# Two changes of order in a loop over routed experts: unit numbers kept in registers, activations cast ahead of rows

## The chip, the cores and the metric

One core of one Trainium2 chip. The metric is the device time of one launch in microseconds (us); smaller is better.

## What is computed

Two layers, each an attention-like block and a feed-forward block with residuals, over `x` of 8 x 256 x 512. The change touches only the last block, a mixture of 32 experts with four picked per token (T = 2048 tokens, H = 512, I = 256), all in 32-bit:

```python
scores = softmax(x @ gate_w.T); topk_w, topk_ids = top_k(scores, 4)   # weights normalized
buf[e, pos] = x[tok]                    # each expert's tokens, up to a capacity
gu = einsum('ech,ehf->ecf', buf, w13);  g, u = split(gu, 2)
act = silu(g) * u
eo = einsum('eci,eih->ech', act, w2)
routed = zeros.at[tok].add(eo[...] * topk_w)
shared = silu(x @ shared_gate_w) * (x @ shared_up_w) @ shared_down_w
out = residual + routed + shared
```

## The kernel before

Everything ahead of the expert loop (both attentions, the first feed-forward block, routing, the shared expert) is as it was and ends near 695 us. Then comes the loop, with a queue of its own written out by hand for each engine; the engines keep step by semaphores alone.

The routed rows are cut into units of 128 rows of one expert; a table in SBUF holds for each unit its expert (in a code that is divided by `STRIDE`) and the column of the row weights. A round handles two units, `s` = 0 and 1, called the first and the second row here. There are 40 rounds; two rounds (`q` = 0 and 1) make one turn of the loop, so rounds are called even and odd. The number of turns is read at run time.

Each 32-bit operand is split into a high part (a cast) and a low part (what the cast lost, `lo_part`, line 1778), and a product is the sum of three: high x high, low x high, high x low.

In round `i`, TensorE does in this order:

- `turn_act(i,0)` (tile `x_ab`, line 2605): transposes the first unit's activation (2 matmuls)
- `turn` of both rows of round `i+1` (tile `x_xb`, line 2587): 8 transposes of the gathered rows
- `down(i,0)` (tile `x_o`, lines 2616, 2617, 2622), with `turn_act(i,1)` between its first products and the others, then `down(i,1)`: 12 matmuls
- `up(i+1,0)` and `up(i+1,1)` (tile `x_h`, lines 2597 to 2599): 12 matmuls each

`up` waits at its head for the low part of the turned row, `down` for the high part of the turned activation, `turn_act` for the activation itself. Which expert's weights a pass uses is in a register of TensorE's queue: `experts_of` loads two unit codes from SBUF (`code_of`, line 1785). A load on a queue is an instruction of that queue; the engine's work is issued by the same queue, ahead of the engine and in order.

ScalarE, per round (`round_of`, line 2731): two silus (line 2712), then `turned_act`, the cast of a turned activation (line 2717), and `turned`, for a turned row: `weigh`, which loads a column number into a register (line 2500) and copies the row's weight (line 2700), and then the row's cast (line 2707). Before the change these stand as activation 0, row 0, activation 1, row 1. At the end both outputs of `down` are copied out of PSUM (line 2747).

VectorE, per round (`round_of`, line 2821): `gated`, silu times up times the row's weight, for each unit (line 2805); the low parts of activation and row, in ScalarE's order; and the split of a new expert's weights where a unit opens one: the first half at the end of a round (`first_half`, lines 2776 and 1778), the second half in the next round between its two `gated` (`second_half`, lines 2782 and 1778). So the second activation of a round stands behind that split.

POOL gathers the rows two rounds ahead (line 1794) and adds the results to memory (line 2521). SP loads the experts' weights two experts ahead (lines 1790 and 1799).

Of the kernel before, what the change touches and what calls it, by code (L numbers as in the profile page):

```python
# [49 lines left out]
NE, TOPK, FI = 32, 4, 256  # L50
# [1675 lines left out]
def experts(nc, st, sem, sbuf, psum, scratch_dram, y_d, a, x, ident, powers, lns, count_row, tail, rows, out):  # L1726
# [50 lines left out]
    def lo_part(dst, src, hi):  # L1777
        return nc.vector.tensor_tensor(dst, src, hi.bitcast(F32), ALU.subtract)  # L1778

    def last_of(eng):  # L1780
        return eng.value_load(last_round[0:1, 0:1], min_val=1, max_val=(T * TOPK // P + NE) // 4 - 1)

    def code_of(eng, j):

        return eng.value_load(unit_tile[0:1, ds(j, 1)], min_val=0, max_val=NE * STRIDE - 1)
# [16 lines left out]
    with ExitStack() as sr:  # L1802
        xl, r, nw, rr, norm = rows.xl, rows.r, rows.nw, rows.rr, rows.norm
# [46 lines left out]
        first = sbuf(sr, "rt_first", [P, 1])  # L1850
# [606 lines left out]
    with ExitStack() as se:  # L2457
# [40 lines left out]
        def column_of(eng, j):  # L2498

            return eng.value_load(unit_col[0:1, ds(j, 1)], min_val=0, max_val=NE)  # L2500
# [81 lines left out]
        def _(pe):  # L2582
            def turn(n, q, s):

                pe.wait_ge(got[q][s], 16 * n + 16)
                for k in range(KD):
                    last = nc.tensor.transpose(xbank[s][:, k * P:(k + 1) * P], xg[q][s][:, k * P:(k + 1) * P], ident[:])  # L2587
                last.then_inc(xt_ps, 1)

            def up(i, s, e):  # L2590

                at = ds(e % SPLIT, 1)
                hi, lo = xt[s]
                pe.wait_ge(w13_lo, e + 1)
                pe.wait_ge(xt_lo, 2 * i + s + 1)
                for k in range(KD):
                    nc.tensor.matmul(hbank[s], hi[:, k, :], w13p[0][:, at, k, :], start=k == 0, stop=False)  # L2597
                    nc.tensor.matmul(hbank[s], hi[:, k, :], w13p[1][:, at, k, :], start=False, stop=False)  # L2598
                    last = nc.tensor.matmul(hbank[s], lo[:, k, :], w13p[0][:, at, k, :], start=False, stop=k == KD - 1)  # L2599
                last.then_inc(h_ps, 1)  # L2600

            def turn_act(i, s):
                pe.wait_ge(x_av_ready, OPEN + 2 * i + s + 1)
                for f in range(KI):
                    last = nc.tensor.transpose(abank[s][:, f * P:(f + 1) * P], av[s][:, f * P:(f + 1) * P], ident[:])  # L2605
                last.then_inc(at_ps, 1)
# [20 lines left out]
            def experts_of(i):  # L2627
                return [code_of(pe, 2 * i + s) // STRIDE for s in range(2)]

            def rest(n, q, e, following=None):  # L2630

                i = 2 * n + q
                turn_act(i, 0)
                if following:
                    turn(n + q, 1 - q, 0)
                    turn(n + q, 1 - q, 1)
                down(i, 0, e[0], between=lambda: turn_act(i, 1))
                down(i, 1, e[1])
                if following:
                    for s in range(2):  # L2640
                        up(i + 1, s, following[s])

            n, first = pe_opens
            for s in range(2):
                up(0, s, first[s])
            with pe.Fori(0, n) as i:
                for q in range(2):
                    rest(i, q, experts_of(2 * i + q), experts_of(2 * i + q + 1))
            rest(n, 0, experts_of(2 * n), experts_of(2 * n + 1))
            rest(n, 1, experts_of(2 * n + 1))  # L2650

            def tile_of(t):
                return banks[t // 2 % 4][:, t % 2]
# [43 lines left out]
        @block.scalar  # L2697
        def _(act):
            def weigh(i, q, s):
                nc.scalar.copy(rw[:, s:s + 1], xg[q][s][:, ds(D + column_of(act, 2 * i + s), 1)]).then_inc(rw_ready, 1)  # L2700

            def turned(i, q, s):
                j = 2 * i + s
                act.wait_ge(xt_ps, OPEN + j + 1)
                act.wait_ge(x_av_ready, OPEN + j - 1)
                weigh(i, q, s)
                nc.scalar.copy(xt[s][0][:], xbank[s].rearrange("p (k n) -> p k n", n=P)).then_inc(xt_hi, 1)  # L2707

            def silu(i, s):
                act.wait_ge(h_ps, 2 * i + s + 1)  # L2710
                act.wait_ge(x_av_ready, OPEN + 2 * i + s - 1)
                nc.scalar.activation(gs[s], hbank[s][:, 0:FI], ACT.Silu).then_inc(gs_ready, 1)  # L2712

            def turned_act(i, s):
                act.wait_ge(at_ps, OPEN + 2 * i + s + 1)
                act.wait_ge(eo_ps, OPEN + 2 * i + s - 1)
                nc.scalar.copy(avt[s][0][:], abank[s].rearrange("p (f n) -> p f n", n=P)).then_inc(at_hi, 1)

            def weights_2(e):
                act.wait_ge(x_w_ready, e + 1)  # L2720
                nc.scalar.copy(w2p[0][:, e], w2[:, e]).then_inc(w2_hi, 1)  # L2721

            act.sem_inc(eo_sb, OPEN)
            weights_2(0)
            act.wait_ge(xt_ps, OPEN + 2)
            nc.scalar.copy(xt[1][0][:], xbank[1].rearrange("p (k n) -> p k n", n=P)).then_inc(xt_hi, 1)
            for s in range(2):
                weigh(0, 0, s)
            weights_2(1)

            def round_of(i, q, more=True, before=None):
                silu(i, 0)
                silu(i, 1)
                turned_act(i, 0)
                if more:
                    turned(i + 1, 1 - q, 0)
                turned_act(i, 1)
                if more:
                    turned(i + 1, 1 - q, 1)
                for s in range(2):  # L2740
                    act.wait_ge(eo_ps, OPEN + 2 * i + s + 1)
                    if not more:
                        nc.scalar.copy(eop[s][0], obank[s]).then_inc(eo_hi, 1)
                        continue
                    if before is not None:
                        act.wait_ge(added[s], 16 * before)
                    nc.scalar.copy(eo[q][s][:], obank[s]).then_inc(eo_sb, 1)  # L2747

            n = last_of(act)
            round_of(0, 0)  # L2750
            round_of(1, 1)
            with act.Fori(0, n - 1) as i:
                round_of(2 * i + 2, 0, before=2 * i + 1)
                round_of(2 * i + 3, 1, before=2 * i + 2)
            round_of(2 * n, 0, before=2 * n)
            round_of(2 * n + 1, 1, more=False)

        @block.vector
        def _(dve):
            def turned(i, s):  # L2760
                dve.wait_ge(xt_hi, 2 * i + s + 1)
                lo_part(xt[s][1][:], xbank[s].rearrange("p (k n) -> p k n", n=P), xt[s][0][:]).then_inc(xt_lo, 1)
# [22 lines left out]
            def split_of(j):  # L2785

                return dve.value_load(unit_split[0:1, ds(j, 1)], min_val=0, max_val=NE - 1)  # L2787
# [8 lines left out]
            def second_half(j, e):  # L2796

                with dve.If(e > 0):
                    dve.wait_ge(eo_ps, OPEN + j - 1)
                    split_2(e)  # L2800
# [7 lines left out]
            def turned_act(i, s):  # L2808
                dve.wait_ge(at_hi, 2 * i + s + 1)
                lo_part(avt[s][1][:], abank[s].rearrange("p (f n) -> p f n", n=P), avt[s][0][:]).then_inc(at_lo, 1)  # L2810

            def gather_rows(r, q):
                nc.vector.tensor_copy(ix[q][:], route[:, 1, ds(2 * r, 2)]).then_inc(ix_ready, 1)
# [7 lines left out]
            def round_of(r, q, more=True, before=None, opening=False, ahead=True):  # L2821

                halves = [] if opening else [(2 * r - 1 + s, split_of(2 * r - 1 + s)) for s in range(2)]
                if ahead:
                    gather_rows(r + 2, q)
                gated(r, 0)
                for j, e in halves:
                    second_half(j, e)
                gated(r, 1)
                turned_act(r, 0)  # L2830
                nexts = [(2 * r + 1 + s, split_of(2 * r + 1 + s)) for s in range(2)] if more else []
                if more:
                    turned(r + 1, 0)
                turned_act(r, 1)
                if more:
                    turned(r + 1, 1)
                if not more:
                    return
                scatter_rows(r, q, before)
                if opening:  # L2840
                    split_13(2)
                    split_2(2)
                for j, e in nexts:
                    first_half(j, e)
# [30 lines left out]
            n = last_of(dve)  # L2875
# [45 lines left out]
```

## Time and profile before

| | |
|---|---|
| median of 3 runs | 1140.03 us (1134.36 to 1140.83) |
| the profiled execution | 1135.46 us, span 1133.6 us, mean granted clock 0.971 |
| TensorE busy | 1058.0 us, 93% of the span |
| VectorE busy | 843.6 us, 74% |
| ScalarE busy | 486.4 us, 43% |
| POOL busy | 444.1 us, 39% |

The span is the profiled execution from its first to its last instruction; its own time is 1.9 us more. The median is 4.6 us above the profiled execution. PE is TensorE's matmuls, PEld its weight loads, which overlap the matmuls; DVE is VectorE, ACT ScalarE; an engine's name with a q (PEldq, ACTq) is the queue that issues its work and also runs its register loads. "issue" as the end of an idle time means that the profile shows no other engine's result that came last. Busy shares are a mean over a program with many stages, so the stage of the change is read by itself.

### The profile page before, as it was taken

What the parts mean: (1) busy time and instruction counts of PE and PEld (TensorE: products, weight loads), DVE (VectorE), ACT (ScalarE), POOL (GpSimd) and SP (SyncE); (2) the same over time, 40 slices, a digit from 0 to 9 for tenths busy, and PEclk for the clock granted to TensorE, in tenths of its full rate; (3) what the DMA queues carried; (4) which work ended last, traced back from release to release, by engine and by line L of the source; (5) the groups of instructions that cost most, each with busy time, mean ns of one, the idle gap of its engine ahead of it and who ended that gap; (6) DMA issues with size and microseconds to landing.
All of it is one profiled execution on the core that took longest, in us unless ns stands there. A gap on an engine that the chain in (4) does not pass through costs nothing. (4 is left out here: it accounts for less than half of the span.)

```text
span 1133.6 us, 21999 instructions
## 1 busy us (share of the span) xinstructions
PE 1058.0 (93%) x6039; PEld 807.7 (71%) x6040; DVE 843.6 (74%) x1588; ACT 486.4 (43%) x1021; POOL 444.1 (39%) x355
## 2 busy tenths in 40 slices
PE   7999789989996999999899989999999999999997
PEld 6999756544443569888787756777777787777763
DVE  5659557969998558778897996868688686866646
ACT  3343235245562269788422073333333333334320
POOL 0000013225541201766861002666566666566620
PEclk9999899999998899989899999999999999999999
DMA  7434540433333587573165315889799899887659
GB/s 280 162 117 176 178 151 3 86 67 70 59 63 77 188 298 253 184 259 123 43 245 189 82 40 195 210 198 262 194 254 258 209 253 257 205 208 185 130 129 359
DMA packets 148190, 195.51 MB, mean 172 GB/s; under 512 B 62985, under 2 KB 80777, under 8 KB 148144
## 3 DMA queue, kind: packets, MB, share of 16 engines
q1 hardware_dynamic: 130512, 156.61, 43.5%
q0 software_dynamic: 17632, 38.32, 16.9%
q8 instruction: 24, 0.39, 0.2%
q14 instruction: 22, 0.18, 0.0%
HBM read 136.56 MB, written 50.34 MB: 165 GB/s over the span
## 5 line engine op out<-in xcount | busy, mean ns | idle before, releaser
L2521 POOL DMA_INDIRECT y_d<-tail,x_ox x78 | 141.3, 1811 | 124.7 <-ACT tail L2747 103.5
L1794 POOL DMA_INDIRECT e_rows<-r_d,x_ix x80 | 105.0, 1312 | 107.0 <-issue 97.7
L2597 PE MATMUL x_h<-x_w_hi,x_t_hi 128*128 x320 | 125.5, 392 | 0.0
L2598 PE MATMUL x_h<-x_w_lo,x_t_hi 128*128 x320 | 125.3, 392 | 0.0
L2599 PE MATMUL x_h<-x_w_hi,x_t_lo 128*128 x320 | 125.0, 391 | 0.0
L1778 DVE TENSOR_TENSOR x_w_lo<-w,x_w_hi (+2 forms) x65 | 112.7, 1734 | 9.3 <-ACT x_w_hi L2721 1.7
L2712 ACT ACTIVATE e_rows<-x_h 128x256 f32<-128x256 f32 x80 | 30.8, 384 | 176.6 <-PE x_h L2599 176.6
L226 POOL TENSOR_TENSOR ln_rstd<-ln_ve,powers 128x2 f32<-128x2 f32 (+1 forms) x40 | 35.3, 883 | 168.1 <-DVE ln_ve L220 168.1
L1778 DVE TENSOR_TENSOR x_t_lo<-x_xb,x_t_hi 128x512 fp32r<-128x512 f32 x79 | 54.6, 692 | 44.2 <-ACT x_t_hi L2707 42.5
L2616 PE MATMUL x_o<-x_w_hi,x_avt_hi 128*128 x160 | 74.0, 463 | 1.1 <-issue 1.1
L1638 DVE SCALAR_TENSOR_TENSOR raw<-h_qk,h_d 128x768 f32<-128x768 f32 x64 | 58.2, 951 | 22.0 <-ACT h_d L1405 9.9
L2597 PEld LDWEIGHTS x_h<-x_w_hi,x_t_hi 128*128 128x128 f32 x320 | 60.5, 189 | 13.3
L2599 PEld LDWEIGHTS x_h<-x_w_hi,x_t_lo 128*128 128x128 f32 x320 | 60.4, 189 | 12.9
L2598 PEld LDWEIGHTS x_h<-x_w_lo,x_t_hi 128*128 128x128 f32 x320 | 60.4, 189 | 12.7
L1404 ACT ACTIVATE h_d<-h_negm,h_g 128x256 f32<-128x256 f32 x128 | 63.6, 497 | 6.9 <-DVE h_negm L1618 3.1
L779 PE MATMUL p_bank<-wo,z_t 128*128 128x512 f32 x128 | 58.3, 610 | 6.9 <-DVE z_t L842 6.9
L2617 PE MATMUL x_o<-x_w_lo,x_avt_hi 128*128 x160 | 63.3, 395 | 0.0
L2805 DVE SCALAR_TENSOR_TENSOR e_rows<-e_rows,x_rw,x_h 128x256 f32<-128x256 f32 x80 | 38.2, 477 | 32.7 <-ACT e_rows L2712 30.3
L1531 PE MATMUL h_pv<-h_v,raw 128*128 128x99 f32 x256 | 55.3, 300 | 0.0
L2747 ACT COPY tail<-x_o 128x512 f32<-128x512 f32 x78 | 46.0, 590 | 18.4 <-PE x_o L2622 18.4
L1532 PE MATMUL h_pv<-h_v,raw 128*128 128x99 f32 x256 | 52.7, 290 | 0.0
L1533 PE MATMUL h_pv<-h_v,raw 128*128 128x99 f32 x256 | 52.3, 288 | 0.0
(434 smaller groups left out, 2665.7 us busy)
## 6 DMA issues: line engine op xcount, KB each, us to landing
w<-in_L_ffn_w SPq DMA_DIRECT2D x32, 1024.0 KB, 9.5
w<-in_L_ffn_w SPq DMA_DIRECT2D x32, 512.0 KB, 8.8
h_negm<-negm_d SPq DMA_DIRECT2D x15, 1024.0 KB, 7.5
raw<-in_L_ffn_w SPq DMA_DIRECT2D x3, 2816.0 KB, 16.1
x_res<-in_x SPq DMA_DIRECT2D x8, 512.0 KB, 5.6
ctx_in<-in_ctx SPq DMA_DIRECT2D x8, 512.0 KB, 3.6
kt_d<-ct SPq DMA_DIRECT2D x8, 512.0 KB, 5.5
vc_d<-ctx_in SPq DMA_DIRECT2D x8, 512.0 KB, 2.6
```

The costliest lines, as they stand in the source:

```text
L779: last = nc.tensor.matmul(p_bank[c][:], zt[:, c, k * P:(k + 1) * P], wo[:, k, :], start=k == 0, stop=k == KD - 1)
L1404: nc.scalar.activation(dm[:, k % 2, j, 0:2, :], nm[:, u, h, 0:2, :], ACT.Exp, bias=gst[:, u, 0, h:h + 1])
L1531: nc.tensor.matmul(pv[:, 0, span, :], c[:, 0:P], near, start=True, stop=True)
L1638: nc.vector.scalar_tensor_tensor(cm[:, k % 2, heads], qk[:, heads, 0:3 * P], float(DH) ** -0.5, dm[:, k % 2, heads].rearrange("p j c n -> ...
L1778: return nc.vector.tensor_tensor(dst, src, hi.bitcast(F32), ALU.subtract)
L1794: nc.gpsimd.indirect_dma_start(out=xg[q][s], out_offset=None, in_=r_d, in_offset=bass.IndirectOffsetOnAxis(ap=ix[q][:, s:s + 1], axis=0), ...
L2521: nc.gpsimd.indirect_dma_start(out=y_d[s], out_offset=bass.IndirectOffsetOnAxis(ap=ox[q][:, s:s + 1], axis=0), in_=eo[q][s][:], in_offset= ...
L2597: nc.tensor.matmul(hbank[s], hi[:, k, :], w13p[0][:, at, k, :], start=k == 0, stop=False)
L2598: nc.tensor.matmul(hbank[s], hi[:, k, :], w13p[1][:, at, k, :], start=False, stop=False)
L2599: last = nc.tensor.matmul(hbank[s], lo[:, k, :], w13p[0][:, at, k, :], start=False, stop=k == KD - 1)
L2616: nc.tensor.matmul(obank[s], hi[:, f, :], w2p[0][:, at, f, :], start=f == 0, stop=False)
L2617: nc.tensor.matmul(obank[s], hi[:, f, :], w2p[1][:, at, f, :], start=False, stop=False)
```

## The change

In TensorE's queue, the two unit numbers that a round is about to use and those of the next are held in four registers over the turns of the loop. Before, each round loaded four unit numbers (its own two and the next round's two) ahead of `turn_act(i,0)`. Now each round loads two, those of the round after the next, between `up(i+1,0)` and `up(i+1,1)`, and at the end of a turn four registers are set from those loaded.

In ScalarE's queue, the casts of both activations come ahead of `weigh` and cast of both rows, and VectorE takes the low parts in the same order. Nothing else of the arithmetic, the tiles or the transfers is changed.

```diff
@@ -2627,7 +2627,7 @@
             def experts_of(i):
                 return [code_of(pe, 2 * i + s) // STRIDE for s in range(2)]
 
-            def rest(n, q, e, following=None):
+            def rest(n, q, e, following=None, after_next=None):
 
                 i = 2 * n + q
                 turn_act(i, 0)
@@ -2637,17 +2637,35 @@
                 down(i, 0, e[0], between=lambda: turn_act(i, 1))
                 down(i, 1, e[1])
                 if following:
-                    for s in range(2):
-                        up(i + 1, s, following[s])
+                    up(i + 1, 0, following[0])
+                    later = experts_of(after_next) if after_next is not None else None
+                    up(i + 1, 1, following[1])
+                    return later
 
             n, first = pe_opens
-            for s in range(2):
-                up(0, s, first[s])
+            held = [nc.alloc_registers(f"x_expert{j}", engines=[mybir.EngineType.PE]) for j in range(4)]
+
+            def hold(j, e):
+                for s in range(2):
+                    nc.regs_mov(held[2 * j + s], e[s])
+
+            def kept(j):
+                return [nc.snap(held[2 * j + s], min_val=0, max_val=NE - 1) for s in range(2)]
+
+            up(0, 0, first[0])
+            second = experts_of(1)
+            up(0, 1, first[1])
+            hold(0, first)
+            hold(1, second)
             with pe.Fori(0, n) as i:
-                for q in range(2):
-                    rest(i, q, experts_of(2 * i + q), experts_of(2 * i + q + 1))
-            rest(n, 0, experts_of(2 * n), experts_of(2 * n + 1))
-            rest(n, 1, experts_of(2 * n + 1))
+                a, b = kept(0), kept(1)
+                c = rest(i, 0, a, b, 2 * i + 2)
+                d = rest(i, 1, b, c, 2 * i + 3)
+                hold(0, c)
+                hold(1, d)
+            a, b = kept(0), kept(1)
+            rest(n, 0, a, b)
+            rest(n, 1, b)
 
             def tile_of(t):
                 return banks[t // 2 % 4][:, t % 2]
@@ -2731,12 +2749,11 @@
             def round_of(i, q, more=True, before=None):
                 silu(i, 0)
                 silu(i, 1)
-                turned_act(i, 0)
-                if more:
-                    turned(i + 1, 1 - q, 0)
-                turned_act(i, 1)
-                if more:
-                    turned(i + 1, 1 - q, 1)
+                for s in range(2):
+                    turned_act(i, s)
+                for s in range(2):
+                    if more:
+                        turned(i + 1, 1 - q, s)
                 for s in range(2):
                     act.wait_ge(eo_ps, OPEN + 2 * i + s + 1)
                     if not more:
@@ -2829,11 +2846,10 @@
                 gated(r, 1)
                 turned_act(r, 0)
                 nexts = [(2 * r + 1 + s, split_of(2 * r + 1 + s)) for s in range(2)] if more else []
-                if more:
-                    turned(r + 1, 0)
                 turned_act(r, 1)
-                if more:
-                    turned(r + 1, 1)
+                for s in range(2):
+                    if more:
+                        turned(r + 1, s)
                 if not more:
                     return
                 scatter_rows(r, q, before)
```

## Rows read from the trace of the kernel before

**Rows 1.** The page: busy time of each engine, share of the span, instructions.
```profile
PE 1058.0 (93%) x6039; PEld 807.7 (71%) x6040; DVE 843.6 (74%) x1588; ACT 486.4 (43%) x1021; POOL 444.1 (39%) x355
```

**Rows 2.** Windows: us, busy PE, PEld, DVE, ACT, POOL, clock, DMA share, GB/s.
```profile
713.91:1092.53 378.62, 374.69 (x1824) 299.51 (x1824) 276.34 (x430) 143.63 (x379) 234.33 (x150) 1.00 0.85 212
813.73:833.64 19.91, 19.73 (x98) 15.75 (x97) 16.76 (x25) 7.59 (x20) 13.50 (x8) 1.00 0.95 257
```

**Rows 3.** Waits of TensorE's weight loads in the loop: total us, times, longest.
```profile
PEld x_o L2616 <- issue: 11.7, 37, 0.6
PEld x_ab L2605 <- issue: 10.9, 19, 1.1
```

**Rows 4.** Line 1785 on TensorE's queue (PEldq), 798 to 805 us.
```profile
L1785 PEldq TENSOR_LOAD <-norm_w x4: 298/538/907, 800.0 to 802.8; - x4
L1785 PEldq SEQ_ASSERT  x4: 18/18/18, 800.6 to 804.0; - x4
```

**Rows 5.** The same line, 808 to 814 us.
```profile
L1785 PEldq TENSOR_LOAD <-norm_w x4: 299/342/586, 810.2 to 812.5; - x4
L1785 PEldq SEQ_ASSERT  x4: 18/18/18, 810.8 to 813.3; - x4
```

**Rows 6.** Timeline of TensorE's matmuls, two openings of a round: start, us.
```profile
803.07 0.39 PE L2599 MATMUL x_h<-x_w_hi,x_t_lo 128*128 x1
804.19 0.43 PE L2605 MATMUL x_ab<-ident,e_rows 128*128 128x128 f32 x2 [0.73 <-issue]
...
813.72 0.39 PE L2599 MATMUL x_h<-x_w_hi,x_t_lo 128*128 x1
813.95 0.38 PE L2605 MATMUL x_ab<-ident,e_rows 128*128 128x128 f32 x2
...
815.61 0.38 PE L2605 MATMUL x_ab<-ident,e_rows 128*128 128x128 f32 x2
```

**Rows 7.** Timeline of TensorE's weight loads, rounds A and B.
```profile
813.50 0.19 PEld L2599 LDWEIGHTS x_h<-x_w_hi,x_t_lo 128*128 128x128 f32 x1
...
815.38 0.37 PEld L2605 LDWEIGHTS x_ab<-ident,e_rows 128*128 128x128 f32 x2
...
816.77 0.19 PEld L2616 LDWEIGHTS x_o<-x_w_hi,x_avt_hi 128*128 128x128 f32 x1 [0.28 <-issue]
...
818.05 0.19 PEld L2597 LDWEIGHTS x_h<-x_w_hi,x_t_hi 128*128 128x128 f32 x1
...
823.26 0.19 PEld L2599 LDWEIGHTS x_h<-x_w_hi,x_t_lo 128*128 128x128 f32 x1
...
825.45 0.36 PEld L2605 LDWEIGHTS x_ab<-ident,e_rows 128*128 128x128 f32 x2
```

**Rows 8.** Line 2500 on ScalarE's queue, 812 to 819 us.
```profile
L2500 ACTq TENSOR_LOAD <-norm_w x2: 284/286/287, 815.0 to 816.3; - x2
```

**Rows 9.** Timeline of ScalarE, round A.
```profile
816.16 0.38 ACT L2717 CAST x_avt_hi<-x_ab 128x256 fp32r<-128x256 f32 x1
816.89 0.19 ACT L2700 COPY x_rw<-e_rows 128x1 f32 x1 [0.35 <-issue]
816.99 0.58 ACT L2707 CAST x_t_hi<-x_xb 128x512 fp32r<-128x512 f32 x1
```

**Rows 10.** Timeline of VectorE, into round A and into round B.
```profile
807.78 0.69 DVE L1778 TENSOR_TENSOR x_t_lo<-x_xb,x_t_hi 128x512 fp32r<-128x512 f32 x1 [0.16 <-ACT x_t_hi L2707]
...
814.57 0.48 DVE L2805 SCALAR_TENSOR_TENSOR e_rows<-e_rows,x_rw,x_h 128x256 f32<-128x256 f32 x1
...
817.60 0.69 DVE L1778 TENSOR_TENSOR x_t_lo<-x_xb,x_t_hi 128x512 fp32r<-128x512 f32 x1 [0.22 <-ACT x_t_hi L2707]
...
824.92 0.48 DVE L2805 SCALAR_TENSOR_TENSOR e_rows<-e_rows,x_rw,x_h 128x256 f32<-128x256 f32 x1
```

**Rows 11.** Line 2776, the first half of an expert's split.
```profile
L2776 DVE CAST x_w_hi<-w x30: 1219/1227/1231, 707.4 to 1057.6; - x29, 128x2048 fp32r<-128x2048 f32 x1
```

## The prediction

> **What bounds the kernel now.** The page first: TensorE is busy 93% of the span, VectorE 74% [rows 1]. The expert loop is its largest single piece: from the first weight load of round 1 (713.91) to that of round 39 (1092.53) lie 378.62 us for 38 rounds, 9.96 each [rows 2]. Two rounds make one turn of the loop, and one such turn takes 19.91 us with TensorE busy 19.73 and VectorE 16.76, the granted clock at 1.00 (2.4 GHz) throughout [rows 2]. What little TensorE lacks is in two places, both called "issue", so no engine's result is shown as late there: 11.7 us in 37 pieces ahead of the first `down` weights, 10.9 us in 19 pieces ahead of `x_ab`, the opening of a round [rows 3].
>
> The timeline tells what each is. I take two rounds and measure from U, the start of the last `up` weight load: round A (odd), U = 813.50, and round B (even), U = 823.26; A takes 9.76 us [rows 7].
>
> *The opening.* In round 10, the last `up` matmul starts at 803.07 and `x_ab` follows at 804.19; in round A the same step takes 0.23 (813.72 to 813.95) [rows 6]. In round 10 TensorE's queue has four register loads, from 800.0 on, the check behind the last at 804.0, and `x_ab` 0.2 later [rows 4]. So the array runs dry because the queue, which issues ahead of it, spends 4 us on four unit numbers. In A the loads start at 810.2 and the last check is at 813.3, before the array's own work ends [rows 5]: no gap. The gap is one of even rounds, 19 in all, where the loop's branch is issued ahead of the loads.
>
> *Ahead of `down(i,1)`.* The cast of the second activation runs 816.16 to 816.54, and `down`'s weights load at 816.77 [rows 7, 9]. The transposes it needs ended at 815.99 (815.61 + 0.38) [rows 6]; ScalarE was in a cast of a row.
>
> **A second bound beside it.** In B VectorE's second `gated` runs 824.92 to 825.40, and the weights for the second `turn_act` load at 825.45, U+2.19 [rows 7, 10]. In A it is 814.57 to 815.05, and the load is at 815.38, U+1.88, where the array is free [rows 7, 10]. So in B the activation is late already, gap or no gap: VectorE came from splitting two experts' halves.
>
> **Part 1: unit numbers in registers.** It takes out two of four loads a round, and moves the other two from the start of a round to between the two `up` passes; it adds four register copies a turn. Their price isn't shown; it lies between nothing and that of the four loads that are gone (0.77 each, below), which made no gap in A, so I take nothing. The 10.9 us go. The array gets back less, for `x_ab` in round 10 opens its round packed closer than in A, and in B the wait for VectorE ends last: taking the gap from B gives nothing while `gated` ends at U+2.14. By itself I give this part 3 to 5 us.
>
> Cover for the moved pair: a weight load follows every (823.26 - 818.05)/23 = 0.227 us in `up`, so the passes that end with the load at 813.50 began at 808.28 [rows 7], and the queue had issued both by 810.2, when it came to its register loads [rows 5]. So the first pass is issued by about +0.96 of the 2.72 that the array takes over it. The register loads follow each other at (812.5 - 810.2)/3 = 0.77 [rows 5], two take 1.53, and the second pass can be issued at about 2.5, 0.2 ahead of need. I cost it at nothing; one load of 0.907 instead of 0.30 [rows 4] breaks that cover by 0.4, and without any cover the pair would cost 1.53 a round.
>
> **Part 2: both activations before both rows.** Gain: the second activation's cast may start at 815.99 + 0.04 instead of 816.16, so 0.13 a round of the 0.3 in front of `down(i,1)`.
>
> Cost: each row's cast on ScalarE stands behind `weigh`, which loads a column number into a register first. Today the first row's `weigh` and cast run while TensorE makes the second activation's transposes. Now they stand behind the wait for those transposes. What does ScalarE's queue do during such a wait? Its second column load in A starts at 816.3, 0.3 behind the transposes' end at 815.99, and `weigh` runs at 816.89, 0.90 behind that end, though the cast before it was over at 816.54 [rows 6, 8, 9]. Load and row operations had been free to go since the first column load at 815.0 was used. So the wait holds the register load as well. The Trainium skill, "Perfetto Trace Analysis", section "DVE / Act Engine Instruction", draws it otherwise: the instruction waits in a wait queue and the sequencer goes on to the next. By that rule the load would be done beforehand; the trace speaks against it here, and it stands as a rival below.
>
> So the first row takes the slot that the second has today: `weigh` U+3.39, cast 3.49 to 4.07, VectorE's low part 4.10 (817.60) to 4.79 [rows 9, 10]. `up(i+1,0)` waits for that low part. From a result to a weight load it is 0.05 (825.40 to 825.45) to 0.23 (816.54 to 816.77) [rows 7, 9, 10]; I take 0.20, nearer to the second, since here too the queue has register work between. `up` starts at U+4.99 instead of 4.55 (818.05) [rows 7]: +0.44, bounds 0.29 to 0.47. The 0.13 won before it is swallowed. A plain round becomes 9.76 + 0.44 = 10.20.
>
> The second row comes one more `weigh` and cast later, 0.60 (the cast alone) to 0.90 (as above); I take 0.90, low part at U+5.02, +0.92. Behind it VectorE has, in 30 rounds, a new expert's first half to split [rows 11], then the first `gated`, the other half's split and the second `gated`: from the low part to that `gated`, 817.60 to 824.92, is 7.32 into an even round, 807.78 to 814.57 is 6.79 into an odd one, at most, for there the silu ended last [rows 10]. With U' = U+10.20, `gated` starts at 5.02 + 7.32 - 10.20 = 2.14 into even and 1.61 into odd rounds, the transposes' weights 0.53 later (2.67 and 2.14), against 1.88: 0.79 and 0.26 late. That delay passes whole through transposes, column load, cast, low part to `up`. It doesn't grow, since VectorE's next chain hangs on the same step. Of the thirty splits 13 lie before even and 17 before odd rounds: 13 x 0.79 + 17 x 0.26 = 14.7 us.
>
> POOL and SP: the copies out of PSUM come 0.4 to 0.9 later, the scatters with them. POOL is busy 13.50 of a turn's 19.91 [rows 2] and fetches rows two rounds ahead, and SP loads two experts ahead, so neither is late next.
>
> **Sum.** 38 x 10.20 + 14.7 = 402.3 against 378.6: +23.7, taken as +23 us. The profiled execution took 1135.5 (span 1133.6), the median of the runs is 1140.0; on the median 1163.
>
> **Rivals.**
> - *VectorE has room (chance 0.15).* `gated` isn't late, or its chain shortens. Then 38 x 10.20 alone, +9, or with the 0.05 latency +3: 1143 to 1149. Against it: B is at its limit today [rows 7, 10].
> - *The pair of loads doesn't fit (0.10).* Loads of 0.9 between the passes: a gap of some 0.3 in each round on top, +11: 1174. For it: four loads had a median of 0.538 in round 10 [rows 4]. Against: those ran some 1 to 3 us later in the round than the moved pair will, and in A the first of the four, which come nearest to the new place, are short.
> - *ScalarE's queue runs ahead of its wait (0.11).* The column numbers are there; a plain round is 9.76 - 0.13 = 9.63, the second low part at U+4.33, `gated` at 2.02 and 1.49: 38 x 9.63 + 13 x 0.67 + 17 x 0.14 = 377.0, -1.6: 1138. The skill's rule gives this one; the 816.3 speaks against it.
> - *TensorE's queue and the cast are all there is (0.09), the faster end.* As the last, and VectorE delivers by U+1.35. It decides at the second row's low part: it would have to start by U+3.66, today it is 4.10. Then 38 x 9.63 = 365.9, -12.7: 1127. For it: both idles are real and TensorE is 99% busy in a turn [rows 2].
>
> **How the numbers follow.** The forecast, 1163, has 0.55. A measurement here can't tell under 1% (11 us) from nothing. Faster by over 1%: the last rival, 0.09. Within 1%: the queue that runs ahead and the VectorE with room, 0.26. Slower: the rest, 0.65. The range leaves out the last two rivals (0.20): from 1143, the low end of the first, to 1175, the pair that doesn't fit.
>
> **What would show it.** Right: no gap between the last `up` and `x_ab` in any round; `up(i+1,0)` at U+5.0 or later with an idle ahead of it of 0.3 or more, released by VectorE's low part; the first row's `weigh` 0.9 behind the transposes; the transposes' second weights at U+2.1 to 2.7 after rounds with a split and 1.9 after the others; turns of 21 to 21.5 us. Wrong: a column load on ScalarE that starts before the transposes end, or a first low part that starts by U+3.5, sinks part 2; TensorE idle between the passes means the fourth case; turns under 19.7 mean the last.

## The result and the profile after

The changed kernel takes 1151.58 us (median of 4 runs, 1150.63 to 1155.29), the kernel before 1138.40 in the same comparison (4 runs, 1134.36 to 1140.83). The ratio is 1.0124, 95% interval 1.0091 to 1.0157: slower by 13 us. The forecast was 1163, in a range of 1143 to 1175. The profiled execution took 1151.63, its span is 1149.8.

The page, busy time of each engine:

```profile
PE 1063.9 (93%) x6039; PEld 799.4 (70%) x6040; DVE 845.6 (74%) x1588; ACT 484.4 (42%) x1021; POOL 450.0 (39%) x355
```

As in [rows 1], it tells nothing: TensorE has 93% before and after. The windows of the loop do, round 1 to round 39 first, then one turn, with the columns of [rows 2]:

```profile
713.35:1109.10 395.75, 384.27 (x1824) 295.89 (x1825) 279.80 (x430) 141.66 (x379) 240.26 (x150) 1.00 0.81 203
816.76:837.73 20.97, 20.24 (x97) 15.52 (x96) 16.81 (x25) 7.47 (x20) 13.36 (x9) 1.00 0.93 245
```

The loop grew from 378.62 [rows 2] to 395.75, by 17.1 us, at the same granted clock; the execution from 1135.5 to 1151.6, by 16.2. So nothing outside the loop needs a cause of its own. A turn takes 20.97 instead of 19.91.

Waits of TensorE's weight loads, 723 to 1105 us:

```profile
PEld x_h L2597 <- issue: 28.9, 72, 0.7
PEld x_ab L2605 <- DVE e_rows L2822: 17.1, 29, 0.9
```

Both places of [rows 3] are gone, the 10.9 us ahead of `x_ab` and the 11.7 ahead of `down`. Two others have come: 28.9 us ahead of `up`'s weights, two pieces a round (one ahead of each pass), and 17.1 ahead of the second activation's transposes, in 29 pieces: the rounds that follow a split.

The timeline of TensorE's weight loads shows them in the rounds that answer to A and B. I call them A' (U = 816.53, 10.32 us) and B' (U = 826.85, 10.66 us, to 837.51):

```profile
816.53 0.19 PEld L2599 LDWEIGHTS x_h<-x_w_hi,x_t_lo 128*128 128x128 f32 x1
...
818.64 0.20 PEld L2605 LDWEIGHTS x_ab<-ident,e_rows 128*128 128x128 f32 x2 [0.32 <-DVE e_rows L2822]
...
821.59 0.19 PEld L2597 LDWEIGHTS x_h<-x_w_hi,x_t_hi 128*128 128x128 f32 x1 [0.63 <-issue]
...
824.42 0.19 PEld L2597 LDWEIGHTS x_h<-x_w_hi,x_t_hi 128*128 128x128 f32 x1 [0.24 <-issue]
...
826.85 0.19 PEld L2599 LDWEIGHTS x_h<-x_w_hi,x_t_lo 128*128 128x128 f32 x1
...
829.45 0.20 PEld L2605 LDWEIGHTS x_ab<-ident,e_rows 128*128 128x128 f32 x2 [0.81 <-DVE e_rows L2822]
...
832.36 0.19 PEld L2597 LDWEIGHTS x_h<-x_w_hi,x_t_hi 128*128 128x128 f32 x1 [0.59 <-issue]
...
837.51 0.19 PEld L2599 LDWEIGHTS x_h<-x_w_hi,x_t_lo 128*128 128x128 f32 x1
```

`up` begins at U+5.06 (821.59), before at U+4.55 [rows 7]. "issue" here is a poor label: what stands just ahead of 821.59 is found on the other engines. ScalarE's timeline in A', its column loads (line 2500), and VectorE's timeline:

```profile
819.12 0.37 ACT L2735 CAST x_avt_hi<-x_ab 128x256 fp32r<-128x256 f32 x1 [1.29 <-PE x_ab L2605]
820.01 0.19 ACT L2718 COPY x_rw<-e_rows 128x1 f32 x1 [0.51 <-issue]
820.10 0.58 ACT L2725 CAST x_t_hi<-x_xb 128x512 fp32r<-128x512 f32 x1
820.89 0.19 ACT L2718 COPY x_rw<-e_rows 128x1 f32 x1 [0.20 <-issue]
820.99 0.58 ACT L2725 CAST x_t_hi<-x_xb 128x512 fp32r<-128x512 f32 x1
```

```profile
L2500 ACTq TENSOR_LOAD <-norm_w x2: 276/288/300, 819.4 to 820.3; - x2
```

```profile
820.72 0.69 DVE L1778 TENSOR_TENSOR x_t_lo<-x_xb,x_t_hi 128x512 fp32r<-128x512 f32 x1 [0.65 <-ACT x_t_hi L2725]
821.60 0.69 DVE L1778 TENSOR_TENSOR x_t_lo<-x_xb,x_t_hi 128x512 fp32r<-128x512 f32 x1 [0.19 <-ACT x_t_hi L2725]
```

The reader is to follow one chain. The row's transposes (line 2587) end at 818.24, the second activation's are at 818.65 and end at 819.09:

```profile
817.20 1.04 PE L2587 MATMUL x_xb<-ident,e_rows 128*128 128x128 f32 x8
...
818.65 0.44 PE L2605 MATMUL x_ab<-ident,e_rows 128*128 128x128 f32 x2
```

Its cast starts at 819.12, the first column load only at 819.4, `weigh` at 820.01 (0.92 behind the transposes, in which ScalarE idles for 0.51), the row's cast at 820.10, its low part at 820.72, which ends at 821.41, and `up` at 821.59. So the row's cast and all behind it in this chain wait for one column number that could have been read earlier, as the experiments show. The load's own waits were over: they are for the row's transposes and for the first `gated`, which VectorE does ahead of the second (818.12). ScalarE's wait for `weigh` is there in every round, twice (723 to 1105 us):

```profile
ACT x_rw L2718 <- issue: 26.0, 74, 0.6
```

### The profile page after: what moved, and what is told of

It is laid out like the page before. It is cut to its first block and busy times, and to the rows that moved or that the text cites. A ratio compares the mean times of both kernels' runs of the same rounds, so it can differ in the third digit from the quotient of the medians.

```text
span 1149.8 us, 21678 instructions
## 1 busy us (share of the span) xinstructions
PE 1063.9 (93%) x6039; PEld 799.4 (70%) x6040; DVE 845.6 (74%) x1588; ACT 484.4 (42%) x1021; POOL 450.0 (39%) x355
## 5 line engine op out<-in xcount | busy, mean ns | idle before, releaser
L2521 POOL DMA_INDIRECT y_d<-tail,x_ox x78 | 145.9, 1871 | 137.1 <-ACT tail L2764 118.4
L2597 PE MATMUL x_h<-x_w_hi,x_t_hi 128*128 x320 | 131.8, 412 | 6.1 <-DVE x_t_lo L1778 5.1
L2616 PE MATMUL x_o<-x_w_hi,x_avt_hi 128*128 x160 | 70.5, 441 | 0.7 <-issue 0.7
L2822 DVE SCALAR_TENSOR_TENSOR e_rows<-e_rows,x_rw,x_h 128x256 f32<-128x256 f32 x80 | 38.2, 477 | 27.7 <-ACT e_rows L2730 25.2
L1778 DVE TENSOR_TENSOR x_avt_lo<-x_ab,x_avt_hi 128x256 fp32r<-128x256 f32 x80 | 33.7, 421 | 32.7 <-ACT x_avt_hi L2735 30.3
L2735 ACT CAST x_avt_hi<-x_ab 128x256 fp32r<-128x256 f32 x80 | 29.7, 371 | 60.3 <-PE x_ab L2605 60.3
L1531 PE MATMUL h_pv<-h_v,raw 128*128 128x99 f32 x256 | 53.5, 292 | 0.0
L1532 PE MATMUL h_pv<-h_v,raw 128*128 128x99 f32 x256 | 51.1, 283 | 0.0
```

What stands on the lines that cost most here:

```text
L1531: nc.tensor.matmul(pv[:, 0, span, :], c[:, 0:P], near, start=True, stop=True)
L2521: nc.gpsimd.indirect_dma_start(out=y_d[s], out_offset=bass.IndirectOffsetOnAxis(ap=ox[q][:, s:s + 1], axis=0), in_=eo[q][s][:], in_offset= ...
L2616: nc.tensor.matmul(obank[s], hi[:, f, :], w2p[0][:, at, f, :], start=f == 0, stop=False)
```

## The experiments

Whole times are medians with the ratio to the kernel before from the same comparison. For the loop I use the window from the opening of round 2 to that of round 39, 37 rounds, since two variants disturb round 1. It is 368.80 us before and 385.93 after, 9.97 and 10.43 a round. Each window is from one profiled execution. Those of the first four kernels stand together here (their lines have the columns of [rows 2]), in this order, one fence each: before, after, registers alone, order alone.

```profile
723.73:1092.53 368.80, 364.87 (x1777) 291.66 (x1776) 268.45 (x419) 140.17 (x370) 228.14 (x146) 1.00 0.84 211
```

```profile
723.17:1109.10 385.93, 374.46 (x1778) 288.13 (x1777) 272.39 (x420) 138.20 (x370) 234.47 (x147) 1.00 0.81 201
```

```profile
725.64:1089.37 363.73, 362.66 (x1778) 292.63 (x1777) 268.36 (x419) 138.31 (x370) 223.94 (x146) 1.00 0.85 214
```

```profile
728.31:1117.95 389.64, 373.99 (x1775) 287.13 (x1776) 272.36 (x419) 141.48 (x370) 231.94 (x146) 1.00 0.81 199
```

### Each part by itself

`pe_only` is the changed kernel with the order of before on ScalarE and VectorE:

```diff
-                for s in range(2):
-                    turned_act(i, s)
-                for s in range(2):
-                    if more:
-                        turned(i + 1, 1 - q, s)
+                turned_act(i, 0)
+                if more:
+                    turned(i + 1, 1 - q, 0)
+                turned_act(i, 1)
+                if more:
+                    turned(i + 1, 1 - q, 1)
...
+                if more:
+                    turned(r + 1, 0)
                 turned_act(r, 1)
-                for s in range(2):
-                    if more:
-                        turned(r + 1, s)
+                if more:
+                    turned(r + 1, 1)
```

> Only the first part of the change: TensorE's unit numbers in registers, two loads between the up passes; ScalarE and VectorE in their order from before. Theory (VectorE's second gated and ScalarE's order set the round): the gap ahead of x_ab goes, but only 3 to 5 us of its 10.9 come back, 1134 us against 1138; turns of 19.6 to 19.8 us. Rival (TensorE's own idle time is the whole bound): 10.9 us come back, 1127 us.

Measured: 1131.74 against 1137.11, ratio 0.9948 (0.9925 to 0.9971). The loop is shorter by 5.1 us. Waits of the weight loads, 723 to 1105:

```profile
PEld x_o L2616 <- issue: 11.0, 32, 0.9
PEld x_ab L2605 <- DVE e_rows L2823: 3.6, 11, 0.5
```

The 10.9 us ahead of `x_ab` are gone, the 11 ahead of `down` have stayed, and 3.6 of a wait have come that was not listed before, for VectorE's second `gated`. About half of the gap is won, a little more than the 3 to 5 us expected.

`order_only` is the kernel before with part 2 alone, the same edit the other way round:

> Only the second part: both activations cast and split ahead of both rows; TensorE loads four unit numbers at the start of a round as before. Theory (the first row's column load waits behind the transposes, so up starts 0.37 us later, and the second gated is late by 0.3 to 0.7 us after a split): the whole loss of the change and the first part's gain on top, +17 to +22 us, 1155 to 1160 us. Rival (the loss came from the pair of loads between the up passes): 1138 us or a little under.

Measured: 1161.03 against 1137.11, ratio 1.0223 (1.0199 to 1.0247), 24 us slower, a little more than expected; the loop +20.8. Its waits, 723 to 1105:

```profile
PEld x_ab L2605 <- issue: 23.8, 36, 1.1
PEld x_h L2597 <- issue: 21.3, 36, 0.6
PEld x_ab L2605 <- DVE e_rows L2804: 7.2, 25, 0.5
```

So the loss is part 2's. Without part 1 it is the larger, for now every round, not every second, has a gap ahead of `x_ab` (36 pieces, 19 before [rows 3]): TensorE's queue is held at the late low part of `up` and loses some of the lead with which it had hidden four loads in odd rounds. In A they start 3.3 ahead of U (810.2, 813.50 [rows 5, 7]), in the round that opens at 843.62 here 3.0 (840.6). One of those four took 0.93, so how much is the lead and how much the longer load was not separated. The two parts add up to +15.8 in the loop; together they are +17.1.

### Is it the order, or the column load?

`after_columns_early` keeps both parts and reads both column numbers at the head of ScalarE's round, where the engine waits for `up`:

```diff
-            def weigh(i, q, s):
-                nc.scalar.copy(rw[:, s:s + 1], xg[q][s][:, ds(D + column_of(act, 2 * i + s), 1)]).then_inc(rw_ready, 1)
+            def weigh(i, q, s, column=None):
+                column = column_of(act, 2 * i + s) if column is None else column
+                nc.scalar.copy(rw[:, s:s + 1], xg[q][s][:, ds(D + column, 1)]).then_inc(rw_ready, 1)
...
             def round_of(i, q, more=True, before=None):
+                columns = [column_of(act, 2 * (i + 1) + s) for s in range(2)] if more else None
```

> The changed kernel with one edit on ScalarE: both column numbers of the next rows are loaded into registers at the head of the round, ahead of the silus; the order of casts stays that of the changed kernel. Theory (the register loads held behind the transposes' wait are what makes the row late): the first low part starts near U+3.6 instead of 4.05, up starts near U+4.4 instead of 4.92, and the second low part near U+4.3; 12 to 17 us under the changed kernel, 1135 to 1140 us. Rival (the loads cost nothing, the casts themselves are late because of their order): up starts still at U+4.8 or later, 1150 us.

Measured: 1127.85 against 1137.11, ratio 0.9935 (0.9911 to 0.9958): faster than before, and some 22 to 24 us faster than the changed kernel (by the ratios or by the medians, which are of two comparisons), where 12 to 17 were expected. `up` starts where the theory had it, and the rival is out. Its loop window, then ScalarE's and VectorE's timelines in the round with U = 811.93, then TensorE's weight load:

```profile
724.45:1084.66 360.21, 359.79 (x1778) 294.12 (x1776) 267.97 (x419) 134.74 (x370) 221.45 (x147) 1.00 0.86 216
```

```profile
814.42 0.38 ACT L2736 CAST x_avt_hi<-x_ab 128x256 fp32r<-128x256 f32 x1 [1.19 <-PE x_ab L2605]
814.69 0.19 ACT L2719 COPY x_rw<-e_rows 128x1 f32 x1
814.78 0.59 ACT L2726 CAST x_t_hi<-x_xb 128x512 fp32r<-128x512 f32 x1
```

```profile
815.40 1.29 DVE L1778 TENSOR_TENSOR x_t_lo<-x_xb,x_t_hi 128x512 fp32r<-128x512 f32 x2
```

```profile
816.32 0.19 PEld L2597 LDWEIGHTS x_h<-x_w_hi,x_t_hi 128*128 128x128 f32 x1
```

`weigh` now follows the cast at once, 0.27 behind its start and not 0.89. The first low part starts at U+3.47 (815.40). `up` starts at U+4.39, with no idle time ahead of it here. The order is the same; only the register loads have moved.

`after_weigh_last` is a second way to the same end. The loads stay in the same part of the round, behind the wait for the transposes, but both `weigh` stand behind both row casts:

```diff
-                weigh(i, q, s)
                 nc.scalar.copy(xt[s][0][:], xbank[s].rearrange("p (k n) -> p k n", n=P)).then_inc(xt_hi, 1)
...
                         turned(i + 1, 1 - q, s)
+                for s in range(2):
+                    if more:
+                        weigh(i + 1, 1 - q, s)
```

> The changed kernel with ScalarE's weigh (column load and copy of the row's weight) of both rows moved behind both row casts; all loads stay, nothing is held in registers. Theory (only what stands between the transposes' wait and the row casts counts): the first low part starts at U+3.6 or a little earlier and the second near U+4.2, up at U+4.4, rounds as with the column numbers early, 1126 to 1130 us. Rival (the order act, act, row, row itself is the loss): up at U+4.8 or later, 1145 us or more.

Measured: 1125.95 against 1135.26, ratio 0.9927 (0.9898 to 0.9955), as expected; the loop 359.10:

```profile
724.23:1083.33 359.10, 358.45 (x1778) 294.35 (x1776) 266.12 (x419) 135.86 (x370) 210.91 (x146) 1.00 0.87 217
```

ScalarE in its round with U = 811.15, and its column loads:

```profile
813.64 0.37 ACT L2734 CAST x_avt_hi<-x_ab 128x256 fp32r<-128x256 f32 x1 [1.19 <-PE x_ab L2605]
813.91 1.08 ACT L2724 CAST x_t_hi<-x_xb 128x512 fp32r<-128x512 f32 x2
814.86 0.21 ACT L2718 COPY x_rw<-e_rows 128x1 f32 x1
815.40 0.19 ACT L2718 COPY x_rw<-e_rows 128x1 f32 x1 [0.33 <-issue]
```

```profile
L2500 ACTq TENSOR_LOAD <-norm_w x2: 280/282/283, 814.1 to 814.8; - x2
```

As many loads of the same length, and the whole loss is gone. The first starts at 814.1, while the two row casts (1.08 together from 813.91) are still under way: behind work whose waits are over the queue does run ahead. In A', behind the cast that waited, it did not.

### The same move on the other two kernels

`before_columns_early` has the edit of `after_columns_early` on the kernel before, `pe_columns_early` has it on `pe_only`:

```diff
+                columns = [column_of(act, 2 * (i + 1) + s) for s in range(2)] if more else None
...
-                    turned(i + 1, 1 - q, 0)
+                    turned(i + 1, 1 - q, 0, columns[0])
...
-                    turned(i + 1, 1 - q, 1)
+                    turned(i + 1, 1 - q, 1, columns[1])
```

> The kernel before with only ScalarE's two column loads moved to the head of the round; TensorE loads four unit numbers at the start of a round. Theory (two bounds side by side, each hides the other): ScalarE's earlier row frees VectorE, but the gap ahead of x_ab in even rounds now shows in full, so 9.65 x 38 + 11 us of gaps, 2 us under the kernel before, 1134 to 1137 us. Rival (the gap was free anyway): 1125 us, as with both edits.

> TensorE's registers as in the changed kernel, the order of before on ScalarE and VectorE (activation 0, row 0, activation 1, row 1), and the column numbers loaded at the head of the round. Theory: the second activation's cast follows its transposes at once, up starts at U+4.4, the second low part at U+3.5, so that the second gated ends before U+1.8 in every round; plain rounds of 9.65 us all through, 366 to 370 us for 38 rounds, 1126 to 1130 us. Rival (VectorE's chain of splits is full whatever the row's time): 1134 us, as with the first part alone.

Measured: `before_columns_early` 1135.27 against 1136.55, ratio 0.9995 (0.9975 to 1.0016), no change that can be told, as expected. `pe_columns_early` 1124.75 against 1137.11, ratio 0.9913 (0.9884 to 0.9943), 1 us better than its range. The first one's waits, 723 to 1105:

```profile
PEld x_ab L2605 <- issue: 16.6, 32, 1.0
```

Its loop takes 366.76, 2.0 less than before. The idle time ahead of the first `down` weights, 12.8 us in this stretch before, falls to 3.1; the one ahead of `x_ab` grows from 10.9 in 19 pieces to 16.6 in 32. Most of what ScalarE gives, TensorE's four register loads take. With the unit numbers in registers the second one's loop comes to 360.00:

```profile
722.40:1082.40 360.00, 358.81 (x1777) 294.64 (x1776) 265.32 (x419) 141.94 (x370) 218.34 (x146) 1.00 0.86 216
```

The same edit is worth 2.0 us in the loop without part 1 and 3.7 with it. And the order makes no difference that these runs can tell once the column loads are out of the way: 360.00 with the order of before, 360.21 with that of after, and the intervals of the whole times overlap.

### VectorE's split taken out

In `after_no_split` (the changed kernel) and `pe_only_no_split`, the split of a new expert inside the loop is cut to 8 columns, so the output uses weights that are not all there; the opening fills the unused slot instead, which delays round 1.

```diff
-                nc.vector.tensor_copy(w13p[0][:, at], w13[:, raw]).then_inc(w13_hi, 1)
-                low_13(e, at, raw)
...
+                nc.vector.tensor_copy(w13p[0][:, at, 0, 0:8], w13[:, raw, 0, 0:8]).then_inc(w13_hi, 1)
+                dve.wait_ge(w13_hi, e + 1)
+                lo_part(w13p[1][:, at, 0, 0:8], w13[:, raw, 0, 0:8], w13p[0][:, at, 0, 0:8]).then_inc(w13_lo, 1)
```

and the same for `split_2`.

> The changed kernel without the splitting of weights in the loop: VectorE touches 8 columns of each half instead of all, so experts from the fourth on use wrong weights; every semaphore and load stays. Theory (the second gated stands behind the split and is what makes the changed kernel's rounds 10.4 and 10.8 us instead of 10.1): all rounds near 10.1 us, gated at U+1.07 everywhere, 10 to 13 us under the changed kernel, 1138 to 1141 us. Rival (VectorE's delay is hidden and the rounds are long for ScalarE's row alone): 1150 us.

> The first part alone, also without the splitting of weights (8 columns of each half, wrong weights from the fourth expert on). Theory: VectorE was the second bound there too, for rounds into even ones: all rounds near 9.72 us, 2 to 5 us under the first part alone, 1127 to 1130 us; what is left ahead of down(i,1) is ScalarE's cast of the row. Rival (no second bound): 1132 us as before.

Measured: `after_no_split` 1146.52, ratio 1.0103 (1.0070 to 1.0136), its loop 375.69; `pe_only_no_split` 1134.05, ratio 0.9976 (0.9952 to 1.0000), its loop 360.90. The loops are to be compared, not the whole times, which came out 4 us and more above both expected ranges: the copies of the opening make round 1 that much longer (its longest wait for VectorE is 5.4 us in `after_no_split` and 5.1 in `pe_only_no_split`).

```profile
728.50:1104.19 375.69, 369.50 (x1777) 290.23 (x1776) 147.62 (x418) 138.40 (x370) 194.77 (x146) 1.00 0.80 205
```

```profile
731.04:1091.94 360.90, 360.74 (x1777) 293.38 (x1776) 143.32 (x418) 138.19 (x370) 194.46 (x146) 1.00 0.83 214
```

VectorE's work is halved (272 to 148), and the changed kernel wins 10.2 us: so much of its loss was the split's chain. Left over is 375.69/37 = 10.154 a round, still 0.19 above the 9.97 of before, though no result of VectorE's split is waited for; its only wait of weight is this one, the column loads':

```profile
PEld x_h L2597 <- issue: 29.3, 73, 0.7
```

In `pe_only` the split is worth 2.8 us: that is about half of the 5.8 us by which part 1 falls short of the 10.9. The other half has no run of its own.

### The best version found

`pe_columns_carry` is `pe_columns_early` with VectorE's split numbers kept in registers too. Each round loaded the codes of two units ahead of the two half-splits and again a round later; now they are loaded once, at the head of the round, and carried:

```diff
-                halves = [] if opening else [(2 * r - 1 + s, split_of(2 * r - 1 + s)) for s in range(2)]
+                nexts = [(2 * r + 1 + s, split_of(2 * r + 1 + s)) for s in range(2)] if more else []
...
+            def hold_split(e):
+                for s in range(2):
+                    nc.regs_mov(carried[s], e[s])
...
+                eb = round_of(2 * i + 3, 1, before=2 * i + 2, halves=of(2 * i + 3, ea))
+                hold_split(eb)
```

> The best version so far (TensorE's registers, order of before, column numbers early) and one more edit on VectorE: the expert numbers of its splits are loaded once, at the head of the round while the engine is busy, and kept in registers for the next round, instead of four loads of which two stand between activation 0 and row 0. Theory: the slow ones of those two loads (0.9 us, some 10 rounds in 38, 4.6 us of waits ahead of the last down weights) go: 3 to 5 us less, 1120 to 1122 us. Rival (they only move a wait): 1125 us.

Measured: 1122.34 against 1136.55, ratio 0.9892 (0.9866 to 0.9919), the lowest of all, though the whole time alone can't tell it from `pe_columns_early`, whose interval it overlaps; the loop is 3.7 shorter, 356.26, 9.63 a round, TensorE busy 356.13 of it, and the 4.6 us ahead of the last `down` weights are no longer listed:

```profile
722.28:1078.54 356.26, 356.13 (x1778) 295.79 (x1776) 276.68 (x420) 142.06 (x370) 221.22 (x146) 1.00 0.87 218
```

## Why the prediction came out as it did

The sign, the place and the mechanism were right; the sum was too large. On the medians the change cost 13 us, little more than half of the 23 forecast. Of the 11.4 us between 1163 and 1151.6, 6.8 are of the sum (+16.2 in the profiled execution, +23 forecast) and 4.6 came from adding to it the distance between the median and the profiled execution of before, which the kernel after doesn't have. In the sum the term that was mis-sized is the delay behind the splits, 14.7 us forecast and 10.2 measured; the plain round has 1.7 of the rest.

- *The opening's gap goes.* Right. No wait ahead of `x_ab` for "issue" is left after.
- *Part 1 alone gives 3 to 5 us, VectorE's second `gated` ends last.* Right in kind: 5.1 in the loop, 5.4 on the medians, at the upper end or just above, and `pe_only_no_split` shows the second bound (2.8 us more).
- *The pair of loads between the `up` passes costs nothing.* Right in its price; the cover that was reckoned is there in `pe_only` and not in the changed kernel. In the latter the loads run from 822.6 to 823.4, 1.0 behind `up`'s start as reckoned, and the check is at 823.9; in `pe_only` they start 0.8 behind it (`up` at 817.75):

```profile
L1785 PEldq TENSOR_LOAD <-norm_w x2: 299/299/299, 822.6 to 823.4; - x2
```

```profile
L1785 PEldq TENSOR_LOAD <-norm_w x2: 295/298/300, 818.6 to 819.4; - x2
```

  There the second pass follows 2.73 behind the first, without idle. In A' it begins at 824.42, 2.83 behind the first, not 2.72, with 0.24 of idle ahead of it, the sign that the forecast named (as "the fourth case"; it means the pair of loads, its second rival). But the passes around that idle run closer. From `up`'s first weights to its last it is 5.26 in A' (821.59 to 826.85) and 5.15 in B' (832.36 to 837.51), before 5.21 [rows 7]; over the 37 rounds of the window the timelines have 5.20 on average after, 5.24 before and 5.23 in `pe_only`. So no price shows.
- *The first row takes the second's slot: `up` at U+4.99, a plain round 10.20.* Right within 0.05: the plain round shown below has U+4.95 (A' has U+5.06, with a split ahead of it), and the round without splits is 10.154. Over 38 rounds that is 15.0 us above 9.76, where the forecast had 16.7. This is the larger part of the loss, and `after_columns_early` and `after_weigh_last` show its cause: with the column load out of the way `up` starts at U+4.4.
- *ScalarE's wait holds the register load behind it.* Right, and the point on which everything hangs. In A' the load starts 0.3 behind the transposes' end (819.09, 819.4), as in [rows 6, 8]. The Trainium skill, "Perfetto Trace Analysis", section "DVE / Act Engine Instruction", has the waiting instruction in a wait queue and the sequencer free for the next; by that rule the load would have been done before 819.09. No run here shows it so. `after_weigh_last` shows how far the queue does run ahead: past casts whose waits are over.
- *The transposes come 0.79 and 0.26 late behind a split, and that passes whole: 14.7 us.* This step failed, in its size. Where they start was right: second weights at U+2.11 in A' (2.14 forecast) and U+2.60 in B' (2.67). But the delay doesn't pass whole. In B' they are 2.60 - 1.88 = 0.72 late, and the round is 10.66 - 10.154 = 0.51 longer; in A' 0.23 late and 0.17 longer. The plain round of `after_no_split` with U = 820.10 shows what is caught up, its weight loads first, then its matmuls:

```profile
820.10 0.19 PEld L2599 LDWEIGHTS x_h<-x_w_hi,x_t_lo 128*128 128x128 f32 x1
...
821.94 0.38 PEld L2605 LDWEIGHTS x_ab<-ident,e_rows 128*128 128x128 f32 x2
...
825.05 0.19 PEld L2597 LDWEIGHTS x_h<-x_w_hi,x_t_hi 128*128 128x128 f32 x1 [0.60 <-issue]
```

```profile
822.18 0.38 PE L2605 MATMUL x_ab<-ident,e_rows 128*128 128x128 f32 x2
```

  On time, the second transposes end 0.62 behind their first weights (821.94 to 822.56), since the matmuls start only 0.24 behind them. Late, they start 0.01 behind and end 0.45 behind (818.64 to 819.09), so 0.17 of the delay is gone there. Over the 37 rounds of the window, against `after_no_split`, the second weights come 0.43 later on average, the transposes' end 0.29, `up` 0.28, and the round is 0.28 longer. That is 15.8 us of delay at the weights, a little above the 14.7 forecast, of which the transposes catch up 5; the splits cost 10.2 us over 37 rounds.
- *The sum.* 15.0 and 10.2 make 25.2. From this goes what the kernel before lost on the same account, for 378.62 is 38 x 9.76 = 370.9 and 7.7 more: 17.5 against 17.1 measured. The forecast made the same subtraction (402.3 - 378.6) with 16.7 and 14.7. The turn shown, 20.97, and two average rounds, 20.86, lie just under the 21 to 21.5 that it named.
- *Readings.* VectorE does not split two experts' halves ahead of B's second `gated`, but the two halves of one expert, the first at the end of A, the second in B; the times stay. The second low part at U+5.02 is 0.92 behind 4.10, though 0.90 was taken: 0.6 us over 30 rounds.
- *What releases `up`.* The forecast named VectorE's low part. The weight loads' wait is listed as "issue", and only TensorE's matmuls name VectorE, with 5.1 us. The timelines of [rows 9, 10] and their like, laid side by side, showed what the label did not.
- *The rivals.* The pair that doesn't fit was wrong by its price: it had 11 us, and none shows. "VectorE has room", 1143 to 1149, comes closer in time (1151.6 is 2.6 above it and 11.4 under the forecast), but its condition isn't met: `gated` is late behind every split, for 17.1 us of waits. The delay was partly caught up elsewhere, in the transposes. The queue that runs ahead, and TensorE's queue and the cast as all there is, are what the kernel would be with the column numbers at hand: 9.63 a round was reckoned for both, `after_columns_early` has 9.735 (360.21/37) and `pe_columns_carry`, with VectorE's loads out of its way as well, 9.63. The first of the two had 11 us of delay by the splits on top (377.0 against 365.9), of which 38 x 9.735 = 369.9 shows 4. The step from 9.735 to 9.63 was not split further: I have not separated the shorter chain on VectorE from the changed place of its loads.

## What to carry to other kernels

A register load stands in its engine's queue like any other instruction, and here it started only when the wait ahead of it was over (819.09, 819.4): put it ahead of the wait, or behind the work that others wait for, and not between the two. When an order is changed, count what comes along with each step that is moved: here the new order was to win 0.13 us a round, and the register load inside the moved step left ScalarE idle in every one (26.0 us in 37 rounds, 0.51 ahead of the first row in A'), on the path to `up`. And where two idles share a path, test the fixes together: the column loads moved ahead gave 2.0 us in the loop alone (nothing that the whole time shows), and 3.7 with the registers.

## What was not expected of the hardware

- One column number costs more than its load: the load is 0.28 to 0.30, but `weigh` starts 0.6 behind the start of the load (819.4 to 820.01). The rest is the register instructions around it:

```profile
L2500 ACTq FUSED_REGOPS  x4: 46/99/152, 819.3 to 820.6; - x4
```

- The loads of VectorE's unit codes in `pe_columns_early` have a median of 0.310 and a longest of 0.991 us, 156 of them in 375 us of loop (the line of its queue, minimum, median and maximum in ns). What makes one three times as long was not found.

```profile
L2807 DVEq TENSOR_LOAD <-unit_split x156: 297/310/991, 702.8 to 1078.1; - x156
```
